# Attention with a delta rule and a mixture of experts in one kernel: another order of a chunk's step on three engines, and scatters that write where they added

## The reference

```python
q, k, v = x @ Wq, x @ Wk, x @ Wv             # 4 heads; dk = 128, dv = 32
beta = sigmoid(x @ Wb); k = k / |k|; q = q * 128 ** -0.5
# delta rule over the 2048 rows of a sequence:
#   delta_t = (v_t - k_t^T S) * beta_t;  S += k_t delta_t^T;  o_t = q_t^T S
o = o * rsqrt(mean(o * o) + 1e-5) * norm_w
x = layernorm(x + (o * silu(x @ Wg)) @ Wo)
# experts: top 2 of 8 by softmax(x @ gate_w^T); per sequence and expert the first
# 640 rows have a slot, later ones are dropped
h = silu(row @ w1[e]) * (row @ w3[e]);  y += p * (h @ w2[e])
x = layernorm(x + y)
```

## Time and profile before

| | us |
|---|---|
| median of 3 runs | 529.44 |
| lowest, highest | 528.06, 533.39 |
| profiled execution | 533.86 |
| its span | 532.1 |
| TensorE, VectorE, ScalarE, GpSimd busy | 474.0, 318.2, 327.8, 325.0 |
| mean granted clock | 0.96 |

### The profile page before, as it was taken

How to read it: one execution, slowest core, us unless ns; L and a number is a source line. 1 busy time by engine, 2 the same in 40 slices (tenths; PEclk the granted TensorE clock), 3 DMA queues, 4 the chain that set the end, 5 groups by cost and what they waited for, 6 DMA issues and landing times.

```text
span 532.1 us, 19041 instructions
## 1 busy us (share of the span) xinstructions
PE 474.0 (89%) x7181; PEld 390.5 (73%) x7181; DVE 318.2 (60%) x1209; ACT 327.8 (62%) x905; POOL 325.0 (61%) x445
## 2 busy tenths in 40 slices
PE   6979988999999999999979877999999999999910
PEld 4656765777667776676656567999999999999910
DVE  4435457767777677767855682654455654555445
ACT  2545767877878778787744643555555555555464
POOL 3052717857688676886865543476676766767752
PEclk9998999999999999999985999999999999999965
DMA  3368754673554835548183224254536545453376
GB/s 94 28 112 201 224 142 51 72 121 40 75 49 60 106 28 74 50 58 107 14 171 41 29 32 111 42 109 56 121 46 129 110 55 109 79 107 35 31 148 198
DMA packets 154804, 46.10 MB, mean 87 GB/s; under 512 B 107168, under 2 KB 149280, under 8 KB 154720
## 3 DMA queue, kind: packets, MB, share of 16 engines
q1 hardware_dynamic: 132848, 29.86, 28.7%
q0 software_dynamic: 20288, 9.51, 19.6%
q10 hardware_dynamic: 1584, 5.59, 2.7%
HBM read 21.39 MB, written 23.55 MB: 84 GB/s over the span
## 4 chain that ended last, share of the span: by engine, by line
PE 44%; POOL 24%; issue 14%; DMA 9%; SPq 4%; DVE 3%; ACT 1%; DVEq 0%; ACTq 0%; POOLq 0%
PE ps L1004 18%; POOL slots_in L1744 11%; PE ps L1015 11%; POOL xs L1727 5%; POOL prod L1726 5%; PE ps L1030 2%; PE ps L681 2%; DMA a_diag<-hb 2%; PE ps L962 2%; POOL silu L1752 1%; SPq L541 1%; DMA inv<-xs 1%; DMA xi<-inv 1%; DMA ssd<-a_diag 1%; DMA xTs<-xT 1%
## 5 line engine op out<-in xcount | busy, mean ns | idle before, releaser
L1785 POOL DMA_INDIRECT x_store<-xk,row x80 | 124.7, 1559 | 66.3 <-ACT xk L1275 46.8
L1744 POOL DMA_INDIRECT slots_in<-x,slot x64 | 99.2, 1550 | 23.7 <-issue 17.1
L1603 DVE TENSOR_TENSOR hb<-ps,hs 128x320 f32<-128x320 f32 (+1 forms) x128 | 62.5, 491 | 47.7 <-ACT hs L1267 43.2
L1267 ACT ACTIVATE hs<-ps 128x320 f32<-128x320 f32 (+1 forms) x128 | 55.3, 435 | 32.1 <-PE ps L1004 27.3
L1004 PE MATMUL ps<-xeTh,w13h 128*128 128x320 f32 x224 | 70.5, 315 | 1.0 <-DVE xeTl L1627 1.0
L1004 PE MATMUL ps<-xeTh,w13l 128*128 128x320 f32 x224 | 69.1, 309 | 0.0
L1004 PE MATMUL ps<-xeTl,w13h 128*128 128x320 f32 x224 | 69.1, 309 | 0.0
L1015 PE MATMUL ps<-w2s,hb 128*128 128x128 f32 x512 | 64.5, 279 | 0.7 <-DVE hb L1603 0.7
L1015 PEld LDWEIGHTS ps<-w2s,hb 128*128 128x128 f32 x512 | 59.8, 192 | 3.1 <-DVE hb L1603 1.1
L1275 ACT ACTIVATE xk<-ps,gs 128x128 f32<-128x128 f32 x80 | 24.2, 364 | 45.0 <-PE ps L1030 35.3
L1726 POOL TENSOR_TENSOR prod<-a,xs 128x28 f32<-128x28 f32 (+11 forms) x120 | 33.3, 278 | 23.8 <-DVE xs L1437 14.9
(11 more groups left out here) (218 smaller groups left out, 1149.4 us busy)
## 6 DMA issues: line engine op xcount, KB each, us to landing
slots_in<-zeros ACTq DMA_DIRECT2D x10, 520.0 KB, 4.0
xe<-slots_in SPq DMA_DIRECT2D x15, 325.0 KB
w<-w_in SPq DMA_DIRECT2D x8, 448.0 KB
xTs<-xT SPq DMA_DIRECT2D x4, 512.0 KB, 5.5
a_diag<-hb SPq DMA_DIRECT2D x64, 32.0 KB
inv<-xs SPq DMA_DIRECT2D x16, 128.0 KB
xi<-inv SPq DMA_DIRECT2D x16, 128.0 KB
xk<-x SPq DMA_DIRECT2D x8, 256.0 KB, 4.3
```

Source lines behind the costliest of these rows:

```text
L1267: af(hs[to, s % 4, :], ps[src, HB[fill_of(s) % 5], 0:HALF], ACT.Silu).then_inc(hs_ready, 1)
L1603: v.tensor_tensor(hb[to, par, c, HALF * g:HALF * g + HALF], ps[rows_, at, 0:HALF], hs[rows_, s % 4, :], ALU.mult).then_inc(h_ready, 1)
L1744: g.indirect_dma_start(out=xs_d[:, :], out_offset=bass.IndirectOffsetOnAxis(ap=to, axis=0), in_=x1[:, p % 2, j, k, :], in_offset=None, com ...
L1785: g.indirect_dma_start(out=x1_d[:, :], in_=ye[:, par, i, :], in_offset=None, out_offset=bass.IndirectOffsetOnAxis(ap=row[:, par, i:i + 1], ...
```

## The change

Three engines get another order of the parts of a step, and one argument goes from the scatter.

```diff
@@ TensorE
                 at(turn_keys, p - 5)
                 at(project, p - 6)
-                at(z_128, p - 5)
                 if p == NP + 5:
                     keep_on(9)
                 key_pair(p - 1, p - 5, 0)
+                at(z_128, p - 5)
+                at(queries, p - 4, 0)
                 at(w_128, p - 5)
-                at(queries, p - 4, 0)
                 at(gate_in, p - 4)
+                key_pair(p - 1, p - 5, 1)
                 at(deltas, p - 5)
-                key_pair(p - 1, p - 5, 1)
                 at(state_queries, p - 5)
+                at(queries, p - 4, 1)
                 at(turn_deltas, p - 5)
-                at(queries, p - 4, 1)
@@ ScalarE
+                at(key_key_out, p - 3, 0)
                 at(z128_copy, p - 7)
-                at(key_key_out, p - 3, 0)
+                at(queries_out, p - 6, 0)
                 at(t128_copy, p - 7)
-                at(queries_out, p - 6, 0)
-                at(deltas_out, p - 7)
                 at(gate_out, p - 6)
                 at(x1_rstd, p - 8)
                 at(key_key_out, p - 3, 1)
-                at(deltas_turned, p - 7)
+                at(deltas_out, p - 7)
...
                 at(queries_out, p - 6, 1)
+                at(deltas_turned, p - 7)
                 at(softmax, p - 8)
@@ VectorE
                 at(state_copy, p - 6)
+                at(gated_values, p - 6)
                 at(z64_copy, p - 5)
-                at(keys_read, p - 5)
-                at(gated_values, p - 6)
                 if p - 6 == NP - 1:
                     w_low(0, 0, 0)
+                at(keys_read, p - 5)
                 at(gated_out, p - 6)
                 if p - 6 == NP - 1:
                     w_low(0, 0, 1)
+                at_group(scale_blocks, p - 2)
+                if p == 2:
+                    solve_first()
                 at(t64_copy, p - 5)
                 at(x64_turned, p - 5)
+                at(masked, p - 5, 0)
                 at(residues, p - 5)
...
-                at_group(scale_blocks, p - 2)
-                if p == 2:
-                    solve_first()
-                at(masked, p - 5, 0)
                 at(normalise, p - 6)
@@ GpSimd, scatter
                         g.indirect_dma_start(out=xs_d[:, :], out_offset=bass.IndirectOffsetOnAxis(ap=to, axis=0),
                                              in_=x1[:, p % 2, j, k, :], in_offset=None,
-                                             compute_op=ALU.bypass if last else ALU.add
                                              ).then_inc(scat_last[j] if last else scat[p % 2], 16)
```

## The result

The changed kernel took **525.85 us** (median of 13 runs, 523.27 to 528.37), beside 528.82 for the kernel before on the same chip (13 runs). The ratio is 0.9935, 95% interval 0.9909 to 0.9961. Run again on two other chips it came to 0.9879 (0.9840 to 0.9919) and 0.9894 (0.9858 to 0.9931). So it is 0.6 to 1.2% faster, 3 to 6 us. The forecast was 515 us, 14 us faster; 525.85 lies just inside the range of 506 to 526, at the end that was kept for the rivals. The profiled execution took 524.84 us (span 523.1, mean granted clock 0.97), against 533.86 and 0.96 before. Three of all executions took 655, 655 and 887 us (the plain writes alone and the kernel before); the means leave them out, and the ratios compare undisturbed executions alone.

The account below looks back on a forecast made before the run. TensorE's ring was taken to pace the steady steps, with GpSimd needing only to be on time. Terms 2.4 + 0.7 + 9.2 + 1.5 + 0.8 = 14.6 us, against the 529.44 us median, gave 515 us; range 506 to 526.

Parts of the forecast that it names:

- the rivals: Alternative outcomes to the forecast, five in all; those at the range's slow end foresaw 523 to 525 us.
- the earlier solve in the tail: Last solve, of chunks 14 and 15: result some 2.4 us sooner, TensorE's wait shrinking from 2.26 to 0.3 to 0.7 us.
- If so, the clock does not fall: Tail: with the wait for the last inverse shrunk, TensorE's clock stays full; the 20.35 us step becomes 13.76, 6.6 us gained.
- the hole: TensorE's idle time between `turn_keys` and `z_128`, some 0.8 us in each step, which the key pair (1.45 us) was to fill.
- Plain writes, 0.59 us each: GpSimd: sixty of 64 scatters lose the addition, each 0.59 us shorter, 2.36 a step, 35.4 us of GpSimd in all.
- The order, 0.4 us a pair, 2.4 in all: Steady steps: the new order on TensorE and VectorE gains near 0.4 us a pair, 2.4 us over six pairs.
- rivals 4 and 5: ScalarE's new order lengthens every step: 525 us with the low clock gone (chance 0.07), 536 with it kept (0.05).
- its bound of 6.4: Worst case of the order: nothing hidden on ScalarE, 0.4 us lost in each of sixteen steps, 6.4 us.
- The early solve, 0.7: Step of chunk 0: the solve of chunks 2 and 3 starts sooner, 0.7 us gained, between 0 and 3.
- The tail, 9.2 and 1.5: Tail: 9.2 us from the shorter wait and the clock staying up, 1.5 from the order in chunks 14 and 15.
- rival 1: Tail: the inverse's two DMAs aren't shortened, a wait above 1 us stays and the clock still falls; 523 us, chance 0.18.
- The end of the stage, 0.8: End of the attention stage: chunk 15's scatters start about 0.8 us sooner, and the loads of the experts' rows follow.

## Why the prediction was wrong

The largest mechanism, the earlier solve in the tail, was right and its size was less than half of what I took: the step that failed there is "If so, the clock does not fall". The steady steps went the other way: the step that failed there is that the key pair "fills" the hole. Against 14.6 us forecast the terms measure 4.0. That 525.85 is inside the range at all is owed to the rivals' end of it, and not to the sum.

1. **Plain writes, 0.59 us each.** Right: 1.55 us became 0.99 on average, 0.56 less. By the Trainium skill's page DMA: Bandwidth & Descriptors, section Anatomy of one DMA, descriptor generation is a small part of a DMA's cost and the receipt of the last write most of it. What the traces measure is the engine's own time: 0.56 us a scatter by the addition, and 0.96 even without it.

2. **The order, 0.4 us a pair, 2.4 in all: wrong in sign.** From chunk 2's `turn_keys` to chunk 12's, ten steps, the changed kernel took 165.7, 166.4 and 166.0 us in its three traces, and the same lists with additions or late weights 167.5 and 166.1. The old order took 162.4 to 165.0 in nine traces (of before and of its variants with other scatters, late weights or added matmuls outside these steps) and 166.3 in the one I worked from. So it costs some 2 us. The step that failed is "Now the key pair (...) fills it". I reckoned TensorE's arrival at the key pair, 0.83 us behind `turn_keys`, and not its operand:

```profile
164.96 1.08 ACT L1070 ACTIVATE y<-ps 128x512 f32<-128x512 f32 x2
165.02 0.44 PE L833 MATMUL ps<-ident,KSt 128*128 128x128 f32 x2
165.29 0.63 PE L902 MATMUL ps<-wox,og 128*128 128x136 f32 x4
166.30 0.61 PE L730 MATMUL ps<-y,xTs 128*64 128x512 f32 x1 [0.37 <-ACT y L1070]
...
169.54 0.68 PE L812 MATMUL ps<-z,x 64*64 64x64 f32 x16 [0.21 <-ACT z L1142]
...
174.67 0.38 ACT L1118 ACTIVATE dl<-ps 128x256 f32<-128x256 f32 x1
175.19 0.64 PE L881 MATMUL ps<-PT,dl 128*32 128x128 f32 x16
```

`keys_out` ends 1.02 us behind `turn_keys`, and the pair starts at 1.28: 0.45 us of the hole stay. `w_128` waits 0.2 for `z128_copy` (I took 0.6 and 0.15; its start, 4.5 us behind `turn_keys`, is near my 4.3). `outputs` waits some 0.2 for `deltas_turned` (I took 0.25). And one cost I had left out: nine products in one piece take 1.27 us, six and three with `w_128` between them 0.91 (an estimate from the spacing of their starts) and 0.55, 0.19 more. Together 1.04, against a hole of 0.8. What the old order does in such a step, with plain writes:

```profile
165.87 0.44 PE L833 MATMUL ps<-ident,KSt 128*128 128x128 f32 x2
166.55 0.73 PE L902 MATMUL ps<-wox,og 128*128 128x136 f32 x4 [0.24 <-DVE og L1465]
167.48 0.68 PE L800 MATMUL ps<-TT,hb 64*64 64x64 f32 x16 [0.19 <-issue]
169.53 0.68 PE L812 MATMUL ps<-z,x 64*64 64x64 f32 x16
```

16.55 against 16.32 us a step. That is the mechanism of rivals 4 and 5 at a third of its bound of 6.4.

3. **The early solve, 0.7.** Not seen: chunk 0's `turn_keys` to chunk 2's takes 33.6 to 35.1 us after, 33.6 to 39.2 with the old order. A spread of that size hides a term of 0.7; a part of it is pauses for "issue" of 1.4 and 2.1 us with the low clock behind them, at 79 and 81 us in two traces of the old order.

4. **The tail, 9.2 and 1.5: less than half.** From chunk 12's `turn_keys` to chunk 15's it was 51.8 and 49.1 us before, and 47.7, 45.9 and 44.6 after: 4.4 on average for my 10.7. "If so, the clock does not fall" failed. It fell in all three traces, for 3.4 to 6.8 us in place of 17.1 and 13.7: behind 2.3 us of "issue"; behind 1.4 for the inverse and 1.3 of "issue"; and behind 2.1 for the inverse. The wait for the inverse, which I reckoned at 0.3 to 0.7 us, was 0.1 in the first of them and 1.4 and 2.1 in the other two: the sum had kept the time of the transfers fixed. The third trace:

```profile
267.52 0.37 SPq L530 DMA_DIRECT2D xi<-inv  x1
272.11 0.29 DVE L1364 TENSOR_SCALAR x32T<-xi,low 128x128 f32<-128x128 f32 x1 [4.22 <-DMA xi<-inv]
272.74 0.72 PE L751 MATMUL ps<-xh,hb 32*32 32x16 f32 x64 [2.07 <-DVE xh L1365]
```

From that load to VectorE's first instruction pass 4.6 us, 4.2 in the second trace, 3.1 in the first and 3.0 before. So in two of the three traces rival 1 came true with its own mechanism, transfers that nothing shortens, and the times of these runs (523.64 and 523.98) are near its price of 523; in the first trace it was another wait, inside `z_64`. Whether the weights' loads slow the transfer, as rival 1 says, stays open: with them a step later it took 4.4. Chunk 12's step, which I said gains nothing, took 14.0 to 15.2 us, against 13.4 to 14.1 in the old order.

5. **The end of the stage, 0.8.** From chunk 15's `turn_keys` to the loads of the experts' rows it takes 22.7 and 22.2 us before, 21.5 with plain writes (0.9 less, as reckoned), 20.5 after: the order gives another 1.0 where ScalarE has no keys to copy. Here it is worth something.

The terms as measured: -2.4 us for the order in the steady steps, +4.4 for the tail and +2.0 for the end of the stage. That is 4.0 of the 4.3 found, and with two to four traces behind each term so near an agreement is partly luck. The tail missed by 6.3 us and the order by 4.8. The terms were also sized on an execution of 533.86 that stands above all but 4 of the 123.

Shown by experiment: that chunk 10's scatters carry the tail's gain, and that the orders of TensorE, ScalarE and VectorE depend on each other. That the order costs is shown by the steps of the traces; by the times alone it is likely. Open: why TensorE stands for "issue" inside a group of products, and why the inverse's transfers differ by 1.6 us from one execution to another.

## What to carry to other kernels

A group that is moved into a hole has an earliest time of its own: look up when its last operand is written, on the engine that writes it, before its duration is counted as a gain. A condition read in a steady step needn't be the one that binds in the last step. And a term that rests on the clock not falling has to count each wait that can come next, since a covered wait of 2 us was followed by another within 5. A path through two transfers has a spread of its own; one trace gives one value of it.

## What the runs showed of the hardware

- An indirect write of 128 rows of 520 bytes that adds holds GpSimd 1.56 us (median of the kernel before), a plain one 0.96 (median of the changed kernel).
- TensorE stood 1.3 to 2.7 us in the middle of groups of matmuls for nothing that a semaphore shows, in five of the traces at 272 to 279 us. Around seven such stalls, these and two at 78 to 81 us, I looked for a 16 KB packet of the queue named "instruction": it lay within 1 us of the start in five, and not in two; two or three are to be expected by chance.
- Waits of 2.1 to 5.0 us for the last inverse were followed by the low level (1.2 in place of 2.4 GHz) in five traces, waits of 1.5, 1.8 and 1.9 us were not by themselves; 1.4 with 1.3 of "issue" 5 us later was. Stalls of 1.4, 1.5 and 1.5 us for "issue" were followed by it as well, and so were waits of 0.4 and 0.8 us close together, so the length of one pause does not tell. The low level of that stretch then lasted from 3 to 17 us.
- From the store of 128 KB to HBM to the load that waits for it passed 3.0 to 4.6 us, and from that load to the first instruction that reads it 2.9 to 4.6, in executions of nearly the same kernel.
